# Low-rank products, the first router and the scan matrix in another order at a kernel's start

## The chip, the cores and the metric

The kernel runs on one core of a Trainium2 chip. The metric is the device time of one execution in microseconds; the median of three runs before is 432.93 us (432.88 to 433.32). One further execution was taken with the profiler; all rows below are of it. Engines are called TensorE (PE, and PEld for its weight loads), VectorE (DVE), ScalarE (ACT), GpSimd (POOL) and SyncE (SP).

## The reference, cut to what matters

```python
xn = layernorm(x)                                    # x: 8 x 256 x 256, float32
x = x + attn0(xn) + ffn0(xn)
xn = layernorm(x)
x = x + attn1(xn) + ffn1(xn)

# ffn0: 8 experts, every one on every token; experts 0 and 1 have a low-rank part
gate = einsum('btd,edf->ebtf', xn, Wg);  up = einsum('btd,edf->ebtf', xn, Wu)
gate[:2] += einsum('btd,edr,erf->ebtf', xn, Ga, Gb)  # the same for up with Ua, Ub; r = 64
mid = silu(gate) * up
out = einsum('ebtf,efd->ebtd', mid, Wd)              # down, with Da, Db for experts 0 and 1
ffn0 = einsum('bte,ebtd->btd', router_weights(xn), out)

# attn0: z = xn @ W.T ; h = z + sum_k eta_k * scan(lam_k, z) ; layernorm(h) * gamma + beta
# router_weights: distance of a sigmoid from 1/e, exponentials, a fallback to the best two
```
attn1 is a gated linear attention with a group norm, ffn1 picks two of 8 experts by token.

## The kernel before

2048 tokens are worked in four groups of 512. All 37 matrices of 256x256 stay in SBUF. For float32 accuracy each is split in two parts: ScalarE copies `w_raw` into the high part `w_hi` (`high`, line 1081), and GpSimd subtracts it to get the low part `w_lo` (`split_low`, line 541, one instruction of 512 columns for each matrix; VectorE does it for the first two, `vector_low`). `w_lo` lies in the place of `w_raw`. Each product is then three matmuls for each piece of the contraction (`passes`, L698). Activations are split likewise: `x_high`/`x_low`, `mid_high`/`mid_low`.

Within a group TensorE runs over e = 0 to 7 (experts in the order 2, 3, 4, 5, 6, 7, 0, 1). `gate_up(g, e, [c])` makes half c of gate and up, 12 matmuls of 512 columns, in PSUM banks G0, U0 or G1, U1. ScalarE applies silu (`silu`), VectorE multiplies by up (`mid_mul`), ScalarE and VectorE split the result (`mid_high`, `mid_low`), and `down(g, e - 1)` runs after `gate_up(g, e)`, 24 matmuls of 256 columns in D0, D1. VectorE adds it, weighted by the router's weight, to `rows` (`down_add`).

Low-rank parts are added to the weights: `lora(i)` (L707) multiplies the two factors into a PSUM bank, VectorE adds that to `w_raw` (`add_lora`, L1750), and only then ScalarE makes the high part. i = 0, 1 (gate0, up0) stand after gate and up of e = 2 in TensorE's stream, i = 2, 3 (gate1, up1) after e = 3, i = 4, 5 (down0, down1) after e = 4; all in M0, M1.

The attention scan of the first layer is a product with a 256-column matrix that VectorE builds at the start of the kernel in four steps (`make_scan_matrix`, each a scan L1714 and a multiply-add L1716, and at the end a cast and a low part): steps 0, 1 ahead of the first `mid_mul`, steps 2, 3 at e = 3. `scan_input` (after `down(0, 4)`) waits for all `lora_added`, `scan` follows at e = 6. `toep_made` marks the matrix done; SyncE's queue waits for it and then loads gamma and clears `sorted_rows` in nine transfers (L454, L459).

At the start TensorE runs 20 warm-up matmuls (L939), transposes x (L719), makes gate and up of the first half in one go (`first_gate_up`, L765 to L771), then the second half, then the router's product (`router_start`, L727), whose transposes (`router_end`, L734) stand in e = 1. VectorE's routing chain (`route_start`, `route_middle`, `route_best`, `route_end`) stands behind `mid_low(0, 0)`. GpSimd's splits are paced by marks: two after x is normed, three after the first part of the scan matrix (`powers_made`), one after `mid_mul` of e = 1, six after `routed`, then beta is added to rows (L560), which waits for `down_add` of e = 2, then six splits, then eight after the next group's x is normed (`x_norm(1)`, at e = 4 on VectorE).

Every engine works its instructions in the order written; the order is by hand, with a semaphore for each step. SyncE's queue issues the transfers of `CHUNKS` in order.

## Time and profile before

| | us |
|---|---|
| median of 3 runs | 432.93 |
| lowest, highest | 432.88, 433.32 |
| the profiled execution's own time | 432.74 |
| its span, first to last instruction | 431.0 |
| TensorE busy | 424.1 |
| VectorE busy | 347.4 |
| ScalarE busy | 177.9 |
| GpSimd busy | 166.2 |

Busy times are sums over the whole span and hide where an engine is the limit. TensorE's are modelled at their ends, so a short stall between two matmuls can't be seen in them; the starts of its weight loads show it.

### The profile page before, as it was taken

The page shows a single profiled execution, that of the slowest core. Times are in us where ns is not written, and L with a number is a line of the kernel's source. Part 1 is how long each engine was busy: PE and PEld are TensorE (multiplying, and loading weights), DVE is VectorE, ACT ScalarE, POOL GpSimd, SP SyncE. Part 2 cuts the span into 40 slices and gives each one's busy share as a digit, 9 for nine tenths or more (in the row PEclk, how much of TensorE's full clock was granted, in tenths as well). Part 3 has the DMA queues.
Part 4 walks back from the last instruction along what each step waited for, and adds up shares of the span by engine and source line. Part 5 has one row for each costly group of instructions (what it writes and reads, how often), then busy time and mean ns, then how long its engine had stood idle before and what let it go on. Part 6 is the DMA issues. An engine that isn't in the chain of part 4 may idle for free.

```text
span 431.0 us, 7493 instructions
## 1 busy us (share of the span) xinstructions
PE 424.1 (98%) x2520; PEld 369.8 (86%) x2520; DVE 347.4 (81%) x1090; ACT 177.9 (41%) x333; POOL 166.2 (39%) x198
## 2 busy tenths in 40 slices
PE   7999999999999999999999999999999999999997
PEld 5788889887888898978988989788999889999886
DVE  6787899998899669889996687989979465856785
ACT  5445445424253725441356234322733333525130
POOL 2417379351017200701072905210441054654656
PEclk9999999999999999999999999999999999999999
DMA  8992499970002130000020310000110844521398
GB/s 286 292 420 92 133 295 285 298 192 0 2 10 89 27 121 1 2 2 1 2 79 19 100 50 0 2 1 2 49 51 24 236 156 122 159 102 50 111 229 261
DMA packets 30166, 46.89 MB, mean 109 GB/s; under 512 B 2680, under 2 KB 24464, under 8 KB 29488
## 3 DMA queue, kind: packets, MB, share of 16 engines
q1 hardware_dynamic: 26064, 36.80, 28.3%
q0 software_dynamic: 3072, 8.80, 6.6%
q10 hardware_dynamic: 992, 0.81, 0.6%
q8 instruction: 21, 0.34, 0.3%
q14 instruction: 17, 0.14, 0.1%
HBM read 22.74 MB, written 23.65 MB: 108 GB/s over the span
## 4 chain that ended last, share of the span: by engine, by line
PE 96%; DVE 2%; DMA 1%; ACT 0%; issue 0%; DVEq 0%
PE D L698 28%; PE G L698 25%; PE U L698 25%; PE M L698 10%; PE M L707 1%; PE D L727 1%; PE M L849 1%; PE M L824 1%; DMA rows<-x 1%; PE M L719 1%; PE D L734 0%; PE M L932 0%; DVE w_lo L1355 0%; DVE stats L1365 0%; PE M L918 0%
## 5 line engine op out<-in xcount | busy, mean ns | idle before, releaser
L698 PE MATMUL D<-w_hi,mid_hi 128*128 128x256 f32 x260 | 74.3, 286 | 0.0
L698 PE MATMUL D<-w_hi,mid_lo 128*128 128x256 f32 x260 | 73.6, 283 | 0.0
L698 PE MATMUL D<-w_lo,mid_hi 128*128 128x256 f32 x260 | 73.5, 283 | 0.0
L1103 ACT ACTIVATE mid<-G 128x512 f32<-128x512 f32 x64 | 37.9, 595 | 76.4 <-PE G L698 66.1
L1476 DVE TENSOR_TENSOR mid<-mid,U 128x512 f32<-128x512 f32 x64 | 43.3, 684 | 25.9 <-PE U L698 14.6
L1490 DVE SCALAR_TENSOR_TENSOR rows<-D,weight,rows 128x256 f32<-128x256 f32 x128 | 54.0, 476 | 4.4 <-PE D L698 4.1
L545 POOL TENSOR_TENSOR w_lo<-w_raw,w_hi 128x512 fp32r<-128x512 f32 x35 | 46.9, 1370 | 27.0 <-ACT w_hi L1076 18.6
L1076 ACT ACTIVATE mid_hi<-mid 128x512 fp32r<-128x512 f32 x64 | 39.9, 630 | 37.5 <-DVE mid L1476 37.2
L1355 DVE TENSOR_TENSOR mid_lo<-mid,mid_hi 128x512 fp32r<-128x512 f32 x64 | 48.3, 774 | 6.1 <-ACT mid_hi L1076 4.6
L698 PEld LDWEIGHTS D<-w_hi,mid_hi 128*128 128x128 f32 x260 | 49.8, 191 | 1.7 <-issue 1.0
L698 PEld LDWEIGHTS D<-w_lo,mid_hi 128*128 128x128 f32 x260 | 49.8, 192 | 0.7
L698 PE MATMUL G<-xT_hi,w_hi 128*128 128x512 f32 x126 | 50.4, 400 | 0.0
L698 PEld LDWEIGHTS D<-w_hi,mid_lo 128*128 128x128 f32 x260 | 49.8, 192 | 0.0
L698 PE MATMUL U<-xT_hi,w_hi 128*128 128x512 f32 x126 | 49.4, 392 | 0.0
L698 PE MATMUL G<-xT_lo,w_hi 128*128 128x512 f32 x126 | 49.3, 392 | 0.0
L698 PE MATMUL G<-xT_hi,w_lo 128*128 128x512 f32 x126 | 49.1, 390 | 0.0
L698 PE MATMUL U<-xT_hi,w_lo 128*128 128x512 f32 x126 | 49.1, 389 | 0.0
L698 PE MATMUL U<-xT_lo,w_hi 128*128 128x512 f32 x126 | 49.0, 389 | 0.0
L625 POOL DMA_INDIRECT sorted_rows<-weighted,slots x24 | 25.2, 1051 | 54.3 <-ACT weighted L1181 48.8
L582 POOL TENSOR_TENSOR scan_part<-scan_part,gamma 128x256 f32<-128x256 f32 x16 | 11.7, 765 | 64.6 <-ACT scan_part L1129 64.6
L698 PEld LDWEIGHTS G<-xT_hi,w_lo 128*128 128x128 f32 x126 | 23.7, 188 | 5.2
L698 PEld LDWEIGHTS U<-xT_hi,w_hi 128*128 128x128 f32 x126 | 23.6, 188 | 5.0
(360 smaller groups left out, 956.4 us busy)
## 6 DMA issues: line engine op xcount, KB each, us to landing
sorted_rows<-weighted SPq DMA_DIRECT2D x8, 1542.0 KB, 18.8
w_raw<-weights SPq DMA_DIRECT2D x5, 1024.0 KB, 18.1
stage<-sorted_rows SPq DMA_DIRECT2D x31, 128.5 KB, 2.3
w_raw<-weights SPq DMA_DIRECT2D x3, 768.0 KB, 11.8
rows<-x SPq DMA_DIRECT2D x7, 256.0 KB, 3.1
part<-rows SPq DMA_DIRECT2D x12, 128.0 KB, 2.0
sums_gate<-part SPq DMA_DIRECT2D x3, 512.0 KB, 6.0
fetched<-returned SPq DMA_DIRECT2D x3, 512.0 KB, 4.8
```

The source lines that it names most:

```text
L545: nc.gpsimd.tensor_tensor(flat, w_raw[:, n, :], w_hi[:, n, :, :].rearrange("p k d -> p (k d)").bitcast(F32), ALU.subtract).then_inc(pool_l ...
L582: nc.gpsimd.tensor_tensor(scan_part[:, t, :], scan_part[:, t, :], gamma[:, :], ALU.mult)\
L625: nc.gpsimd.indirect_dma_start(sorted_rows[:, :], bass.IndirectOffsetOnAxis(slots[:, q, j:j + 1], 0), weighted[j][:, t, :], None).then_inc ...
L698: ins = nc.tensor.matmul(out_ap, a, b, start=(first and n == 0), stop=(last and n == 3 * len(pairs) - 1))
L707: ins = nc.tensor.matmul(LORA_PS[i][:, k * D:(k + 1) * D], a[:, k * P:(k + 1) * P], b, start=True, stop=True)
L719: ins = nc.tensor.transpose(MT[k][:, t * P:(t + 1) * P], ln[:, t, k * P:(k + 1) * P], ident[:, :])
L727: ins = nc.tensor.matmul(bank[0:2 * E, :], routers[:, layer, k, :, :].rearrange("p a e -> p (a e)"), part[:, k, :], start=n == 0, stop=n = ...
L1076: return nc.scalar.activation(o, i, ACT.Copy)
L1103: nc.scalar.activation(mid[:, c, :], GU[2 * c][:, :], ACT.Silu).then_inc(silu_ready, 1)
L1355: return v.tensor_tensor(o, i, hi.bitcast(F32), ALU.subtract)
L1476: v.tensor_tensor(mid[:, c, :], mid[:, c, :], GU[2 * c + 1][:, :], ALU.mult)\
L1490: ins = v.scalar_tensor_tensor(rows[g % 2][:, t, :], DN[t // 2][:, (t % 2) * D:(t % 2 + 1) * D], weight0[:, t, ORDER[e]:ORDER[e] + 1], row ...
```

## The change

TensorE runs 12 warm-ups, then the low-rank products i = 0 to 3 into G1, U1, D0, D1. ScalarE copies them from there into `w_raw` (`hold_lora`), and GpSimd's queue adds the weights onto them by two accumulating transfers. VectorE's adds remain for i = 4, 5, now both at e = 5 as before; the products of down stay after e = 4 on TensorE. The factors of gate and up are loaded ahead of the weights. The first router's product stands between first gate and first up product, its transposes behind the up product. VectorE's routing chain up to `route_best` stands ahead of `mid_low(0, 0)`; the scan matrix is made at e = 3 (steps 0, 1) and e = 4 (steps 2, 3). GpSimd's splits: 2, 3, 4; the two transfers; 5, 6 after `route_best` (`picks_made`); 7 to 13 after `routed`; beta; 14 to 17; 18 on after x of the next group is normed.

```diff
-CHUNKS = ((0, 1), (1, 2), (2, 4), (4, 5), (5, 8), (8, 10), (10, 13), (13, 17), (17, 21), (21, 25), (25, 28),
-          (28, 32), (32, 36), (36, 37))
+LORA_HELD = 4
+JOINED = tuple((WHERE[f"gate{_e}"], WHERE[f"gate{_e}"] + 2) for _e in range(2))
+CHUNKS = ((0, 1), (1, 2), (2, 4), (4, 5), (5, 8), (8, 10), (10, 13), (13, JOINED[0][0]), JOINED[0],
+          (JOINED[0][1], JOINED[1][0]), JOINED[1], (JOINED[1][1], 28), (28, 32), (32, 36), (36, 37))
-WARMUPS = 20
+WARMUPS = 12
-        LORA_PS = [M0, M1, M0, M1, M0, M1]
+        LORA_PS = [G1, U1, D0, D1, M0, M1]
@@ SyncE
             load_x(sp, 0, 0)
+            load_gu(0)
+            load_gu(1)
             for c in range(6):
                 load_chunk(c)
...
             for c in range(7, len(CHUNKS)):
-                load_chunk(c)
+                if CHUNKS[c] not in JOINED:
+                    load_chunk(c)
@@ GpSimd
             pool.wait_ge(xn_act_ready, 2)
             split_low(2, 4)
-            pool.wait_ge(powers_made, 1)
-            split_low(4, 7)
-            pool.wait_ge(mid_ready, at(0, 2 * E, 2 * 1 + 2))
-            split_low(7, 8)
+            split_low(4, 5)
+            for e in range(2):
+                first, end = JOINED[e]
+                pool.wait_ge(lora_held, 2 * (e + 1))
+                nc.gpsimd.dma_start(w_raw[:, first:end, :], weights[:, first:end, :], accum_op=ALU.add)\
+                    .then_inc(chunk_loaded[CHUNK_OF[first]], 16)
+            pool.wait_ge(picks_made, 1)
+            split_low(5, 7)
             pool.wait_ge(routed, 1)
-            split_low(8, 14)
+            split_low(7, 14)
...
-            split_low(14, 20)
+            split_low(14, 18)
             pool.wait_ge(xn_ready, at(1, 2, 2))
-            split_low(20, WHERE["o"])
+            split_low(18, WHERE["o"])
@@ TensorE
+            for i in range(LORA_HELD):
+                if i % 2 == 0:
+                    pe.wait_ge(lora_gu_loaded[i // 2], 16)
+                lora(i)
             pe.wait_ge(const_made, 5)
             transpose_x(0)
-            first_gate_up()
-            gate_up(0, 0, [1])
+            first_product(0)
             pe.wait_ge(routers_ready, 1)
             router_start(M0, 0, xT_hi, xT_lo, (logitT_ps[0], 1))
+            first_product(1)
+            router_end(M0, 0, 0)
+            pe.wait_ge(lora_held, 2)
+            gate_up(0, 0, [1])
...
-                    if g == 0 and e == 1:
-                        router_end(M0, 0, 0)
...
-                    if g == 0 and e == 2:
-                        pe.wait_ge(logit0_ready, 1)
-                        pe.wait_ge(lora_gu_loaded[0], 16)
-                        for i in (0, 1):
-                            lora(i)
-                    if g == 0 and e == 3:
...
+                    if g == 0 and e == 1:
+                        pe.wait_ge(lora_held, LORA_HELD)
...
                     if e == SCAN_AT[g]:
-                        pe.wait_ge(lora_added, LORA)
+                        pe.wait_ge(lora_added, LORA - LORA_HELD)
@@ ScalarE
+            def hold_lora(i):
+                act.wait_ge(lora_ps, i + 1)
+                copy(w_raw[:, WHERE[LORA_NAMES[i]], :], LORA_PS[i][:, :]).then_inc(lora_held, 1)
...
             high(0)
+            x_norm(0)
             high(1)
-            x_norm(0)
+            x_high(0)
             high(2)
-            x_high(0)
             high(3)
+            hold_lora(0)
             silu(0, 0, 0, mid_used=False)
+            hold_lora(1)
+            logits_out(0, 0)
             high(4)
+            hold_lora(2)
+            hold_lora(3)
+            route_start(0)
+            silu(0, 0, 1, mid_used=False)
+            route_exp(0)
             high(5)
-            silu(0, 0, 1, mid_used=False)
             high(6)
-            logits_out(0, 0)
             for c in range(KC):
                 mid_high(0, 0, c)
-            route_start(0)
             silu(0, 1, 0)
-            route_exp(0)
@@ VectorE
             vector_low(1)
-            make_scan_matrix((0, 1))
             mid_mul(0, 0, [0])
+            route_start(0, M0)
+            route_middle(0)
             mid_mul(0, 0, [1])
+            route_best(0)
+            v.memset(carrier[:, :], 0.0).then_inc(picks_made, 1)
             mid_low(0, 0)
-            route_start(0, M0)
             mid_mul(0, 1, [0])
-            route_middle(0)
-            route_best(0)
             mid_mul(0, 1, [1])
...
-                        if first and e in (3, 4, 5):
-                            add_lora(2 * e - 6)
-                            add_lora(2 * e - 5)
+                        if first and e == 5:
+                            for i in range(LORA_HELD, LORA):
+                                add_lora(i)
...
-                    if g and e == 1:
+                    if e == 1:
                         route_end(g)
...
-                    if first and e == 1:
-                        route_end(g)
...
-                    if first and e == 3:
-                        make_scan_matrix((2, 3))
+                    if first and e in (3, 4):
+                        make_scan_matrix((2 * e - 6, 2 * e - 5))
```

## Rows read from the trace of the kernel before

**Rows 1.** The page, its part 1: busy time, share of the span, instructions.
```profile
PE 424.1 (98%) x2520; PEld 369.8 (86%) x2520; DVE 347.4 (81%) x1090; ACT 177.9 (41%) x333; POOL 166.2 (39%) x198
```

**Rows 2.** Waits of TensorE, 0 to 110 us: total us, times, longest.
```profile
PE U L768 <- DVE w_lo L1355: 0.5, 1, 0.5
```

**Rows 3.** Timeline of weight loads: start us, us, instruction, idle before.
```profile
31.40 0.19 PEld L698 LDWEIGHTS U<-xT_lo,w_hi 128*128 128x128 f32 x1
31.63 0.19 PEld L698 LDWEIGHTS U<-xT_hi,w_lo 128*128 128x128 f32 x1
32.17 1.59 PEld L707 LDWEIGHTS M<-gu_factors 64*128 64x128 f32 x8 [0.35 <-issue]
34.09 0.19 PEld L698 LDWEIGHTS D<-w_hi,mid_hi 128*128 128x128 f32 x1 [0.33 <-issue]
...
42.63 1.59 PEld L707 LDWEIGHTS M<-gu_factors 64*128 64x128 f32 x8 [0.35 <-issue]
```

**Rows 4.** Timeline of all engines, 0 to 14 us.
```profile
1.53 6.46 PE L939 MATMUL D<-xT_lo 128*128 128x512 f32 x20 [1.53 <-DVE xT_lo L1757]
...
7.24 0.63 ACT L1076 ACTIVATE w_hi<-w_raw 128x512 fp32r<-128x512 f32 x1 [0.73 <-DMA w_raw<-weights]
...
7.94 1.09 ACT L1136 ACTIVATE ln<-rows,shift,rstd 128x256 f32<-128x256 f32 x2
...
10.19 0.96 PE L765 MATMUL G<-xT_hi,w_hi 128*128 128x512 f32 x2 [0.34 <-ACT xT_hi L1076]
...
11.28 1.69 DVE L1355 TENSOR_TENSOR w_lo<-w_raw,w_hi 128x512 fp32r<-128x512 f32 x1
```

**Rows 5.** DMA issues: KB each, us to landing; first one issued at 1.34.
```profile
w_raw<-weights SPq DMA_DIRECT2D x1, 256.0 KB, 4.0
...
sums_gate<-returned POOLq DMA_DIRECT2D x3, 512.0 KB, 10.7
```

**Rows 6.** Timeline of VectorE, first and last instruction of the choosing part.
```profile
23.76 0.20 DVE L1438 TENSOR_SCALAR den_e<-th_e 128x64 f32<-128x64 f32 x1 [0.41 <-ACT th_e L1123]
...
26.80 0.23 DVE L1407 TENSOR_TENSOR picked<-expert_id,top_f 128x64 f32<-128x64 f32 x1
```

**Rows 7.** Timeline of VectorE, 42 to 89 us.
```profile
42.81 0.69 DVE L1476 TENSOR_TENSOR mid<-mid,U 128x512 f32<-128x512 f32 x1 [0.71 <-PE U L698]
...
44.80 0.69 DVE L1714 TENSOR_TENSOR_SCAN carry_gain<-small_in,carry_gain 128x256 f32<-128x256 f32 x1
...
47.62 0.42 DVE L1355 TENSOR_TENSOR toep_lo<-gamma,toep_hi 128x256 fp32r<-128x256 f32 x1
...
50.55 0.69 DVE L1476 TENSOR_TENSOR mid<-mid,U 128x512 f32<-128x512 f32 x1 [0.93 <-PE U L698]
51.15 1.28 DVE L1750 TENSOR_TENSOR w_raw<-w_raw,M 128x512 f32<-128x512 f32 x2
...
54.25 3.07 DVE L1355 TENSOR_TENSOR mid_lo<-mid,mid_hi 128x512 fp32r<-128x512 f32 x2
...
59.79 1.21 DVE L1330 TENSOR_SCALAR rstd<-newton 128x4 int32<-128x4 int32 x1
...
73.22 1.61 DVE L1735 TENSOR_TENSOR_SCAN carry_gain<-small_in 128x255 f32<-128x255 f32 x1
...
87.84 0.68 DVE L1355 TENSOR_TENSOR mid_lo<-mid,mid_hi 128x512 fp32r<-128x512 f32 x1
```

**Rows 8.** Timeline of weight loads: the first of the last down product.
```profile
88.70 0.19 PEld L698 LDWEIGHTS D<-w_hi,mid_hi 128*128 128x128 f32 x1
```

**Rows 9.** Timeline of GpSimd, 50 to 75 us: the two batches of splits.
```profile
52.54 8.44 POOL L545 TENSOR_TENSOR w_lo<-w_raw,w_hi 128x512 fp32r<-128x512 f32 x6
63.31 10.97 POOL L545 TENSOR_TENSOR w_lo<-w_raw,w_hi 128x512 fp32r<-128x512 f32 x8 [2.34 <-DVE ln L1375]
```

**Rows 10.** Timeline of SyncE's queue and of ScalarE: clearing transfers, first use.
```profile
48.46 40.19 SPq L459 DMA_DIRECT2D sorted_rows<-weighted  x9
...
125.69 2.07 ACT L1181 ACTIVATE weighted<-rows,row_shift,row_gain 128x256 f32<-128x256 f32 x4
```

More of the change, by code:

```diff
@@ L755, in scan, with first_product @@
                                   (*now, yT_hi[:, 1, :], yT_lo[:, 1, :])]).then_inc(h_ps, 1)
-            def first_gate_up():
-                for up in range(2):
-                    n = WHERE[NAMES[up]]
-                    cols = slice(0, P)
-                    for k in range(KC):
-                        pe.wait_ge(high_ready, n + 1)
-                        pe.wait_ge(xT_hi_ready, k + 1)
-                        nc.tensor.matmul(GU[up][:, :], w_hi[:, n, k, cols], xT_hi[:, k, :], start=k == 0, stop=False)
-                    for k in range(KC):
-                        pe.wait_ge(vector_low_ready, n + 1)
-                        nc.tensor.matmul(GU[up][:, :], w_lo[:, n, k, cols], xT_hi[:, k, :], start=False, stop=False)
-                    for k in range(KC):
-                        pe.wait_ge(xT_lo_ready, k + 1)
-                        ins = nc.tensor.matmul(GU[up][:, :], w_hi[:, n, k, cols], xT_lo[:, k, :], start=False,
-                                               stop=k == KC - 1)
-                    ins.then_inc(gu_ps, 1)
+            def first_product(up):
+                n = WHERE[NAMES[up]]
+                cols = slice(0, P)
+                for k in range(KC):
+                    pe.wait_ge(high_ready, n + 1)
+                    pe.wait_ge(xT_hi_ready, k + 1)
+                    nc.tensor.matmul(GU[up][:, :], w_hi[:, n, k, cols], xT_hi[:, k, :], start=k == 0, stop=False)
+                for k in range(KC):
+                    pe.wait_ge(vector_low_ready, n + 1)
+                    nc.tensor.matmul(GU[up][:, :], w_lo[:, n, k, cols], xT_hi[:, k, :], start=False, stop=False)
+                for k in range(KC):
+                    pe.wait_ge(xT_lo_ready, k + 1)
+                    ins = nc.tensor.matmul(GU[up][:, :], w_hi[:, n, k, cols], xT_lo[:, k, :], start=False,
+                                           stop=k == KC - 1)
+                ins.then_inc(gu_ps, 1)
             def gate_up(g, e, chunks=range(KC), between=None):
@@ L938, in _ @@
             for _ in range(WARMUPS):
-                nc.tensor.matmul(D1[:, :], xT_lo[:, 0, 0:P], xT_lo[:, 0, :], start=True, stop=True)
+                nc.tensor.matmul(M0[:, :], xT_lo[:, 0, 0:P], xT_lo[:, 0, :], start=True, stop=True)
+            for i in range(LORA_HELD):
+                if i % 2 == 0:
+                    pe.wait_ge(lora_gu_loaded[i // 2], 16)
+                lora(i)
             pe.wait_ge(const_made, 5)
             transpose_x(0)
-            first_gate_up()
-            gate_up(0, 0, [1])
+            first_product(0)
             pe.wait_ge(routers_ready, 1)
             router_start(M0, 0, xT_hi, xT_lo, (logitT_ps[0], 1))
+            first_product(1)
+            router_end(M0, 0, 0)
+            pe.wait_ge(lora_held, 2)
+            gate_up(0, 0, [1])
             def unit(u, owners):
@@ L976, in group @@
                         scan(g)
-                    if g == 0 and e == 2:
-                        pe.wait_ge(logit0_ready, 1)
-                        pe.wait_ge(lora_gu_loaded[0], 16)
-                        for i in (0, 1):
-                            lora(i)
-                    if g == 0 and e == 3:
-                        pe.wait_ge(lora_added, 2)
-                        pe.wait_ge(lora_gu_loaded[1], 16)
-                        for i in (2, 3):
-                            lora(i)
-                    if g == 0 and e == 4:
-                        pe.wait_ge(lora_added, 4)
-                        pe.wait_ge(lora_down_loaded, 16)
-                        for i in (4, 5):
-                            lora(i)
+                    if g == 0 and e == 1:
+                        pe.wait_ge(lora_held, LORA_HELD)
                     if e == 1:
                         pe.wait_ge(logit0_ready, at(g, 1, 1))
+                    if g == 0 and e == 4:
+                        pe.wait_ge(lora_down_loaded, 16)
+                        for i in range(LORA_HELD, LORA):
+                            lora(i)
                     if g and e == 3:
@@ L1717, in make_scan_matrix @@
                                                  gamma[:, :] if k else unit, ALU.mult, ALU.add))
-                if SCANS - 1 not in scans:
-                    v.memset(carrier[:, :], 0.0).then_inc(powers_made, 1)
-                else:
+                if SCANS - 1 in scans:
                     setup(v.tensor_copy(toep_hi[:, :], gamma[:, :]))
@@ L1782, in group @@
                             unit_low(0)
-                        if first and e in (3, 4, 5):
-                            add_lora(2 * e - 6)
-                            add_lora(2 * e - 5)
+                        if first and e == 5:
+                            for i in range(LORA_HELD, LORA):
+                                add_lora(i)
                         if first and e == NORM_AT[g]:
```

9 lines of the change are left out of this document (4 added, 5 removed).

## The prediction

> **What bounds the kernel now.** I read the page first: TensorE is busy for 424.1 of 431.0 us, 98%, the others for 81% and less [rows 1]. So an edit gains only by what it takes out of TensorE's own stream, or out of a wait of TensorE. The list of waits of TensorE over the first 110 us, read next, holds four entries, all before 14 us; the one the change aims at is the wait of the first up product for its low part [rows 2]. Then the weight loads in order of time: in dense stretches they follow at 0.23 us for 512 columns with no hole (31.40, 31.63) [rows 3], and this is how a stall is seen, since a matmul's modelled end hides it. Last, VectorE beside GpSimd from 42 to 89 us. There VectorE is idle only once, for 0.93 us, and its last low part of the last expert ends at 88.52, 0.18 us ahead of the down product that needs it at 88.70 [rows 7, 8]. VectorE is thus a second bound, just hidden, in the very stretch from which the change takes TensorE work.
>
> **Low-rank products of gate and up put first.** They stand in the dense stream now: a last product load at 31.63, the eight passes from 32.17, the next down product at 34.09. That is 2.46 us where 0.23 would do, so 2.23 us a time; the second time has the same shape, 1.59 us of loads after a 0.35 us hole [rows 3]. Both go: **-4.46 us** of TensorE. The third pair (down) stays.
>
> **The head.** Warm-ups fall from 20 (1.53 to 7.99) to 12, so they end near 7.99 - 8 x 0.227 = 6.2 [rows 4]. The factors are now loaded ahead of the first two weight chunks and should land where these did, 1.34 + 4.0 = 5.3 and 7.24 [rows 4, 5]; the four products, 16 passes of 0.2 to 0.23, run from about 6.4 to 9.8. The first chunk, two places later in the queue, lands near 7.9, so ScalarE's norm ends at 9.55 instead of 9.03, and then the eight transposes wait for TensorE itself: the first matmul moves from 10.19 to 11.2 (between 10.6 and 11.6). On the other side the wait in the up product goes: its low part came at 12.97, late because VectorE needed 1.69 us for an instruction that takes 0.68 elsewhere [rows 2, 4, 7], a hole of 0.8 us together with its refill. The router's four matmuls now fill it. Head: +1.0 - 0.8 = **+0.2** (-0.4 to +0.7). If the products were free and nothing else moved, the sum would be -4.26. The copies that hold the products (four of 0.6 on ScalarE, as its copy at 7.24 in [rows 4]) fit between its other work: the logits copy ends at 14.8, the router's transposes come at 15.2.
>
> **Weights added by DMA.** The two transfers of 512 KB from GpSimd's queue are like the three late ones, which landed in 10.7 us [rows 5]; issued near 17 they may take twice that under the weight loads and are wanted by ScalarE near 45. Nothing, and 1 to 1.5 us of GpSimd while it would wait anyway. They spare VectorE four adds of 0.64.
>
> **Routing chain ahead.** Let T be the start of the first expert's second half on TensorE. Its 12 matmuls take 2.7, VectorE starts 0.5 after the last (42.81 against a stream that ended 0.31 ahead of 42.63, by the hole in [rows 3]), multiplies 0.6, and runs the choosing part, now in front of the low parts: 23.76 to 27.03, 3.3 us [rows 6]. Then two low parts of 0.65: T+8.4. TensorE wants them after 36 matmuls, T+8.2. So 0.3 us are lost even undisturbed. But the mark that lets GpSimd go on is set right before them, and GpSimd's next split takes its turn between the two: +1.03, the time VectorE stood still behind one split at 59.79 (1.21 for an instruction of 0.17) [rows 7]. **+1.35** (0 to 2.4: with the first also blocked). In the kernel before this chain stood behind the low parts.
>
> **The scan matrix moved.** This is the term that decides. Start the clock when the fourth expert's up product is through: VectorE starts at 42.81, TensorE needs the last low part at 88.70. TensorE's distance, 45.89, becomes 45.89 - 2.23 = **43.66**, since the second pair of products stood right behind that point. VectorE's way, 42.81 to 88.52, is 45.71. Out of it come the 0.93 of idle time and one pair of adds, 1.28 (the pair before lies ahead of 42.81) [rows 7]. The second half of the scan matrix, 44.80 to 47.96 or 3.16, moves one expert later; the first half takes its place and came from the head: 3.16 less the casts plus one small step, 2.68. Undisturbed VectorE needs 45.71 - 0.93 - 1.28 + 2.68 = 46.2 and meets TensorE's 43.7: 2.5 us late, with 0.1 of slack in between.
>
> **Turns with GpSimd.** From [rows 7] I take a rule of this trace: while GpSimd runs its splits back to back, a VectorE instruction on two SBUF operands waits for the split in progress, then GpSimd waits its turn. Two low parts took 3.07 for 1.28, a small step 1.21, a scan over 255 columns 1.61 for 0.69. Products read from PSUM did not wait (the adds of products, 1.28 for two, beside GpSimd's beta sum). Before, the batch of six splits [rows 9] cost VectorE 1.8 in the low parts and 1.2 in the norm. Now it is four splits, and they meet the low parts and the moved half of the scan matrix, eight such instructions in a row: 0.25 + 4 x 1.03 = 4.4, against 3.0: +1.4. The second batch grows from eight [rows 9] to ten, and reaches into the carry gain's last step and the next low parts: +1.3. Together +2.7; the bounds are -1.7 (the moved scans don't wait, four of the waits gone, the second batch as before) and +4. So VectorE arrives 2.5 + 2.7 = **5.2 us** late (0.8 to 6.5). TensorE would pay it mostly in front of the scan's input product, which waits until VectorE has added the two down products, and the rest at the last down product.
> The rows show turns. The Trainium skill ("SBUF — State Buffer", SBUF: two separate sides) states it as an exclusive lock on a pair of ports, held for a whole instruction, against VectorE work with two SBUF inputs or in a two-port mode; it speaks against moving scans beside the splits. By that rule the sum stands as above; were it not so, the term would be 2.5 or less.
>
> **Behind the scan matrix on SyncE's queue**: its mark comes near 60 instead of 48, and the clearing transfers wait for it. They are issued from 48.46 for 40.19 us and end near 102; now near 114. ScalarE first needs them at 125.69 [rows 10]. Nothing; if the margin of 11 us were gone, as much as it is overrun.
>
> **Sum**: -4.46 + 0.2 + 1.35 + 5.2 = +2.3. The profiled execution took 432.74 (431.0 of span and 1.7 around it), the median of the runs is 432.93, so it is a usual one: 432.74 + 2.3 = **435.0**.
>
> **Rivals.**
> First, that is the case above: VectorE and its turns set group 0's end. For it: one idle time in 46 us; the 0.18 us at 88.52. Chance 0.48, 433.8 to 437.
> Second, **the turns don't grow**, the change is faster. Place: the low parts and the moved scans, 50 to 58 us. Price: with the contention of before less the norm's 1.2, VectorE is 1.3 late, the first low parts cost 0.3: -4.46 + 0.2 + 0.3 + 1.3 = -2.7, 430.1; with contention simply unchanged 2.5 and -1.5, 431.3. It decides once VectorE's extra waiting stays under 0.9 us in all. For it: the splits are held back until the norm is done. Against: scans waited at 73.22. Chance 0.27.
> Third, between them: half of the added waiting, the low parts as costed: -4.46 + 0.2 + 1.35 + 3.5 = +0.6, 433.3. Chance 0.16.
> Fourth, **no stall at all**, VectorE had hidden slack: -4.26, 428.5. Against it the idle time of 0.93. Chance 0.04.
> Fifth, the head goes wrong: the factors land late, TensorE stands between the shorter warm-ups and the products, and runs the first products at 1.2 instead of 2.4 GHz. The warm-ups stood 0.32 apart on average where dense matmuls of their size stand 0.227 apart [rows 3, 4]; some 12 matmuls at half the pace cost 12 x 0.227 = 2.7 more, 437.7. Chance 0.05.
>
> **How the numbers follow.** 0.2% of the time, 0.87 us, is about what a measurement can tell from no change: faster is below 432.1, slower above 433.8. Faster takes the second and fourth and a little of the third, 0.32; same 0.18; slower 0.50, the first and fifth less a margin. For 8 in 10 the range leaves out the fourth and the far end of the fifth: 430.2 to 437.0. The likeliest case alone is 433.8 to 437.0.
>
> **What would show each step.** The passes of the low-rank products before 10 us, none at 32 and 42. The first product's start near 11.2 and no hole in the up product. A hole of about 1.3 us in front of the first down product (near 24) and a wait of it for VectorE's low parts. Scan instructions of 1.3 to 1.7 us instead of 0.7 between 50 and 60; a wait of the scan's input product of 2 to 3 us for VectorE's adds; later a second one at the last down product. VectorE without idle time from there to 90. I am wrong if TensorE's stream has no holes after 15 us, or if VectorE's scans keep 0.69.

## The result, and the profile after

| | before | after |
|---|---|---|
| median of the runs, us | 433.02 (432.85 to 433.45, 8 runs) | 435.42 (434.75 to 436.93, 8 runs) |
| ratio to before | | 1.0061 (95%: 1.0044 to 1.0077) |
| the profiled execution, its span | 432.74, 431.0 | 436.93, 435.1 |

The change makes the kernel slower by 0.6%. The forecast was 435.0. The profiled execution of the changed kernel is the slowest of its runs. Five of its runs lie at 434.75 to 435.54 and three at 436.43 to 436.93; the difference has a place in the trace, shown at the end of this section.

The page, part 1 (busy time, share of the span, instructions): TensorE is busy 1.0 us less than in [rows 1], in a span 4.1 us longer.

```profile
PE 423.1 (97%) x2512; PEld 369.7 (85%) x2512; DVE 348.8 (80%) x1086; ACT 179.8 (41%) x337; POOL 172.1 (40%) x200
```

Waits of TensorE, 0 to 110 us (total us, times, longest), against [rows 2]. The wait of the up product for its low part is gone. Waits for VectorE's low parts and for its added weights, 5.5 us together, stand in its place.

```profile
PE D L706 <- DVE mid_lo L1365: 3.2, 2, 2.1
PE M L706 <- DVE w_raw L1758: 2.3, 1, 2.3
```

Timeline of weight loads (start us, us, instruction, idle before), against [rows 3] and [rows 8]:

```profile
6.75 0.73 PEld L715 LDWEIGHTS G<-gu_factors 64*128 64x128 f32 x4 [0.45 <-issue]
...
8.26 1.05 PEld L715 LDWEIGHTS D<-gu_factors 64*128 64x128 f32 x5
9.64 0.85 PEld L727 LDWEIGHTS M<-ident,ln 128*128 128x128 f32 x8 [0.33 <-issue]
11.04 0.19 PEld L771 LDWEIGHTS G<-xT_hi,w_hi 128*128 128x128 f32 x1 [0.55 <-issue]
...
23.37 0.19 PEld L706 LDWEIGHTS U<-xT_hi,w_lo 128*128 128x128 f32 x1
25.04 0.19 PEld L706 LDWEIGHTS D<-w_hi,mid_hi 128*128 128x128 f32 x1 [1.48 <-issue]
...
63.34 0.19 PEld L706 LDWEIGHTS D<-w_hi,mid_lo 128*128 128x128 f32 x1
66.05 0.19 PEld L706 LDWEIGHTS M<-w_hi,xT_hi 128*128 128x128 f32 x1 [2.52 <-DVE w_raw L1758]
...
87.75 0.90 PEld L727 LDWEIGHTS M<-ident,ln 128*128 128x128 f32 x8
90.96 0.19 PEld L706 LDWEIGHTS D<-w_hi,mid_hi 128*128 128x128 f32 x1 [2.32 <-issue]
```

The four low-rank products of gate and up stand in front of the transposes now, and none of them is in the dense stream. Three long holes are new. Read from the load before to the load behind, less one spacing (0.23 for 512 columns, 0.12 in a down product, 0.87 for the eight transposes, which is the distance when nothing waits), they are 25.04 - 23.37 - 0.23 = 1.44 at the first down product, 66.05 - 63.34 - 0.12 = 2.59 at the scan's input product, and 90.96 - 87.75 - 0.87 = 2.34 at the last down product. Two small ones of 0.21 and 0.22 stand at 60.61 and 84.88.

Timeline of VectorE, against [rows 7], and below it the splits of GpSimd, against [rows 9]:

```profile
22.54 0.69 DVE L1365 TENSOR_TENSOR mid_lo<-mid,mid_hi 128x512 fp32r<-128x512 f32 x1
23.15 1.77 DVE L1365 TENSOR_TENSOR mid_lo<-mid,mid_hi 128x512 fp32r<-128x512 f32 x1
...
42.09 0.69 DVE L1486 TENSOR_TENSOR mid<-mid,U 128x512 f32<-128x512 f32 x1 [2.03 <-PE U L706]
...
51.03 2.60 DVE L1365 TENSOR_TENSOR mid_lo<-mid,mid_hi 128x512 fp32r<-128x512 f32 x2
53.55 1.78 DVE L1724 TENSOR_TENSOR_SCAN carry_gain<-small_in,carry_gain 128x256 f32<-128x256 f32 x1
55.37 1.33 DVE L1726 SCALAR_TENSOR_TENSOR gamma<-carry_gain,small_in,gamma 128x256 f32<-128x256 f32 x1
56.73 1.66 DVE L1724 TENSOR_TENSOR_SCAN carry_gain<-small_in,carry_gain 128x256 f32<-128x256 f32 x1
58.43 0.48 DVE L1726 SCALAR_TENSOR_TENSOR gamma<-carry_gain,small_in,gamma 128x256 f32<-128x256 f32 x1
...
64.72 1.28 DVE L1758 TENSOR_TENSOR w_raw<-w_raw,M 128x512 f32<-128x512 f32 x2
...
78.41 1.83 DVE L1365 TENSOR_TENSOR mid_lo<-mid,mid_hi 128x512 fp32r<-128x512 f32 x2
...
90.21 0.68 DVE L1365 TENSOR_TENSOR mid_lo<-mid,mid_hi 128x512 fp32r<-128x512 f32 x1
```

```profile
22.70 3.37 POOL L549 TENSOR_TENSOR w_lo<-w_raw,w_hi 128x512 fp32r<-128x512 f32 x2 [4.43 <-DVE carrier L1779]
...
51.34 6.51 POOL L549 TENSOR_TENSOR w_lo<-w_raw,w_hi 128x512 fp32r<-128x512 f32 x4
64.29 13.85 POOL L549 TENSOR_TENSOR w_lo<-w_raw,w_hi 128x512 fp32r<-128x512 f32 x10 [6.45 <-DVE ln L1385]
```

A low part of 0.69 takes 1.77 while GpSimd's first split runs (22.70), scans of 0.69 take 1.78 and 1.66, a multiply-add of 0.48 takes 1.33. The multiply-add at 58.43, just behind the batch of four (51.34 + 6.51 = 57.85), takes its bare 0.48.

Last, the granted clock, by stretches (length, then busy time of TensorE, its loads, VectorE, ScalarE and GpSimd, then the clock as a share of 2.4 GHz, DMA share, GB/s). First the profiled execution above, then another one of the same kernel, which took 434.67 us (it is the first run of the next section).

```profile
85.00:90.00 5.00, 3.88 (x33) 3.64 (x32) 4.78 (x10) 3.78 (x9) 2.99 (x4) 1.00 1.10 264
90.00:95.00 5.00, 4.01 (x22) 4.04 (x23) 4.47 (x10) 0.35 (x1) 4.56 (x7) 0.68 1.10 273
```

```profile
65.00:70.00 5.00, 4.55 (x25) 4.56 (x26) 5.00 (x9) 2.21 (x4) 5.00 (x4) 0.66 1.13 259
...
90.00:95.00 5.00, 4.60 (x32) 4.34 (x33) 4.93 (x12) 0.43 (x2) 5.00 (x7) 1.00 1.13 259
```

In both, a piece of a 5 us stretch runs at 1.2 instead of 2.4 GHz, right behind a hole. In the first execution it lies behind the last hole: the last down product runs from 90.96 to 95.31, 4.35 us, where the other execution needs 2.86 (90.37 to 93.23). In the second it lies behind the hole of the scan's input product, where VectorE is the bound: TensorE only arrives later at the last hole, which shrinks from 2.34 to 0.96. The mean granted clock over a whole run is on record for every run: 0.995 or 0.996 in all twelve of the changed kernel. So the clock falls in each of them, and what sets the two groups apart is, as it seems, where it falls; the place is traced in these two only.

### The profile page after: what moved, and what is told of

Same layout as the page of the kernel before. It is cut to its first block, busy times and chain, and to the rows that moved or that the text cites. A ratio compares the mean times of both kernels' runs of the same rounds, so it can differ in the third digit from the quotient of the medians.

```text
span 435.1 us, 7473 instructions
## 1 busy us (share of the span) xinstructions
PE 423.1 (97%) x2512; PEld 369.7 (85%) x2512; DVE 348.8 (80%) x1086; ACT 179.8 (41%) x337; POOL 172.1 (40%) x200
## 4 chain that ended last, share of the span: by engine, by line
PE 86%; DVE 12%; issue 1%; ACT 1%; DVEq 0%
PE D L706 25%; PE G L706 21%; PE U L706 21%; PE M L706 8%; DVE mid_lo L1365 2%; DVE rows L1500 2%; PE D L735 1%; PE M L945 1%; DVE mid L1486 1%; PE M L855 1%; DVE carry_gain L1724 1%; PE M L830 1%; DVE gamma L1726 1%; DVE carry_gain L1743 1%; PE M L727 1%
## 5 line engine op out<-in xcount | busy, mean ns | idle before, releaser
L549 POOL TENSOR_TENSOR w_lo<-w_raw,w_hi 128x512 fp32r<-128x512 f32 x35 | 50.1, 1464 | 25.6 <-ACT w_hi L1078 11.4
L1365 DVE TENSOR_TENSOR mid_lo<-mid,mid_hi 128x512 fp32r<-128x512 f32 x64 | 50.4, 808 | 4.7 <-ACT mid_hi L1078 3.3
```

Source lines behind the costliest of these rows:

```text
L549: nc.gpsimd.tensor_tensor(flat, w_raw[:, n, :], w_hi[:, n, :, :].rearrange("p k d -> p (k d)").bitcast(F32), ALU.subtract).then_inc(pool_l ...
L1365: return v.tensor_tensor(o, i, hi.bitcast(F32), ALU.subtract)
```

## The experiments

Every median below stands beside runs of the kernel before on the same chip; these lay between 433.07 and 433.12, except for the last kernel. Each ratio is to them, with its 95% interval in brackets. Where an expectation gives the last hole as 1.6 to 1.8, that was counted with too wide a spacing for the transposes; by the spacing of 0.87 used above it is 2.34.

**The changed kernel once more.** No edit.

> The changed kernel once more, nothing edited. Theory A (VectorE sets the end of group 0, through its own work and its turns with GpSimd): holes of 1.4 us before the first down product, 2.6 before the scan's input product and 1.8 before the last down product, in this trace too, within 0.1 each. Theory B, about the spread of the runs (434.75 to 436.93): the granted clock fell behind the last hole in the profiled run (0.68 over 90 to 95 us, where the last down product took 4.3 us instead of 2.9), a dip of some executions only. Then a run near 435 shows the same holes without that dip, and one near 436.8 shows it; the two kinds lie about 1.5 us apart.

435.59 us (434.65 to 436.61), 1.0064 [1.0041, 1.0088]. The holes are those above: 1.44, 2.59, and at the end

```profile
88.54 0.90 PEld L727 LDWEIGHTS M<-ident,ln 128*128 128x128 f32 x8
...
90.37 0.19 PEld L706 LDWEIGHTS D<-w_hi,mid_hi 128*128 128x128 f32 x1 [0.93 <-issue]
```

The result repeats, with two runs at 434.7 and two at 436.5. I had expected a run near 435 to have no fall of the clock and the same last hole. It has the fall, behind the scan's input product, and a smaller last hole (0.96).

**The scan matrix away from GpSimd's splits.** All four steps in the fourth expert, the first two ahead of its low parts.

```
+                        if first and e == 3:
+                            make_scan_matrix((0, 1))
...
-                    if first and e in (3, 4):
-                        make_scan_matrix((2 * e - 6, 2 * e - 5))
+                    if first and e == 3:
+                        make_scan_matrix((2, 3))
```

> The changed kernel with the scan matrix one place earlier: steps 0 and 1 between the two halves of the fourth expert (e = 3), where VectorE stood idle for 2.0 us, steps 2 and 3 behind that expert's low parts, as in the kernel before. Theory A: VectorE gets back 3.2 us at e = 4 and three waits for splits of about 1 us each, and is late by some 0.6 us at the start; the holes before the scan's input and the last down product shrink from 4.6 together to 0.5 or less, and the time falls by 4 to 5.5 us to 430 to 431.4. Rival C (the holes come from the added products' wait or the second batch of splits, whichever place the matrix has): the first of them may go, the one before the last down product stays near 1.8, and the time stays above 433.

432.82 us (432.1 to 433.3), 0.9992 [0.9982, 1.0001]. That is 2.8 less than the changed kernel, from the order of the same instructions alone. Timeline of VectorE, and the loads at the last down product:

```profile
45.30 0.68 DVE L1724 TENSOR_TENSOR_SCAN carry_gain<-small_in,carry_gain 128x256 f32<-128x256 f32 x1
46.02 0.48 DVE L1726 SCALAR_TENSOR_TENSOR gamma<-carry_gain,small_in,gamma 128x256 f32<-128x256 f32 x1
```

```profile
85.18 0.90 PEld L727 LDWEIGHTS M<-ident,ln 128*128 128x128 f32 x8
88.03 0.19 PEld L706 LDWEIGHTS D<-w_hi,mid_hi 128*128 128x128 f32 x1 [1.95 <-issue]
```

The steps have their bare times and the hole of 2.59 is gone. But the last hole still stands at 1.98: TensorE arrives there 2.6 us sooner (transposes at 85.18, in the changed kernel at 87.75), and VectorE 2.9 (the load at 88.03, there at 90.96). From the weights it adds at the scan's input to its last low part VectorE needs 25.0 us here (63.00 to 87.96), 24.9 in the changed kernel (66.00 to 90.89) and 23.5 in the kernel before (65.02 to 88.52). That stretch is the one beside the second batch of splits, ten where [rows 9] has eight, and this run leaves it alone. So the gain at the scan's input is carried to the end of the group whole, and what was lost behind it stays lost; I had expected 1.4 to 2.8 us more. In all ten runs the mean clock is 0.999 or 1.0: the fall is absent.

**The low parts ahead of the choosing part.** The first low parts in front of the routing chain.

```
             mid_mul(0, 0, [1])
+            mid_low(0, 0)
             route_best(0)
             v.memset(carrier[:, :], 0.0).then_inc(picks_made, 1)
-            mid_low(0, 0)
```

> The changed kernel with the low parts of the first expert ahead of the choosing part of the routing chain, as in the kernel before; all else as changed. Theory A: the hole of 1.4 us before the first down product goes, the rest keeps its size, since VectorE has 4 us of idle time at e = 3 to start the scan stretch afresh: -1.4, near 434.0. Rival C (the time that this hole cost is made up by later holes, for VectorE is the bound from the start on): the later holes grow by as much and the time stays at 435.4.

435.62 us (434.18 to 436.37), 1.005 [1.0032, 1.0068], where 434.0 was expected. The 1.44 went, and a hole of 0.87 came one product later:

```profile
32.48 0.19 PEld L706 LDWEIGHTS D<-w_hi,mid_hi 128*128 128x128 f32 x1 [0.92 <-issue]
```

Here half of the idle time is a wait for the adds of the first down product (0.5), which need the routing weights. The chain is wanted as early as the low parts are, and neither order serves both. The scan hole (idle 2.52) and the last (2.31) stayed. The 0.6 us less of holes can't be seen in the median of five runs that spread over 2.2.

**Splits 5 and 6 held until the first low parts are through.**

```
             pool.wait_ge(picks_made, 1)
+            pool.wait_ge(mid_lo_ready, 2)
             split_low(5, 7)
```

> The changed kernel with GpSimd's splits 5 and 6 held until VectorE's low parts of the first expert are done; VectorE's and TensorE's order untouched. It prices the turn in the first hole. Theory A: the second low part, 1.77 us in the changed kernel, takes 0.69 again and the hole before the first down product falls from 1.4 to 0.3 to 0.4. The time falls by up to 1.1, less what the later splits cost in route_end (a wait of about 1 us as in the kernel before, covered by VectorE's idle time at e = 3). 434.3 to 435. Rival D (low parts are slow for another cause): 1.77 stays.

434.70 us (434.21 to 435.7), 1.0036 [1.0023, 1.0048]. The first hole falls from 1.44 to 0.34, with one of 0.31 at the next down product: both low parts take 0.69. So 1.1 of the 1.44 was the one turn of GpSimd, as the prediction split it (1.03 and 0.3).

**Two of the four splits held until the scan matrix is done.**

```
-            split_low(14, 18)
+            split_low(14, 16)
+            pool.wait_ge(toep_made, 1)
+            split_low(16, 18)
```

> The changed kernel with GpSimd's last two splits before the norm (14 to 17 in one batch now) held until the scan matrix is done; VectorE's order is untouched. It prices the turns alone. Theory A: two of the three waits of 0.9 to 1.1 us in the moved scan steps go, VectorE's scan ends about 2 us earlier and the hole before the scan's input product falls from 2.6 to 0.6 to 1.0; -2 us, 433.3 to 433.7. Rival D (the long scan instructions have another cause, memory traffic of the weight loads say, or the splits only move into the norm and cost as much there): scans stay at 1.3 to 1.8 us or the norm's small steps lengthen, and the time stays within 0.5 of 435.4.

434.71 us (434.41 to 435.42), 1.0036 [1.0023, 1.0048]. Timeline of VectorE:

```profile
53.49 1.78 DVE L1726 TENSOR_TENSOR_SCAN carry_gain<-small_in,carry_gain 128x256 f32<-128x256 f32 x1
...
55.83 0.69 DVE L1726 TENSOR_TENSOR_SCAN carry_gain<-small_in,carry_gain 128x256 f32<-128x256 f32 x1
...
59.73 0.75 DVE L1341 TENSOR_SCALAR newton<-mv 128x4 f32<-128x4 f32 x1
```

Two waits are gone (0.85 and 0.97), one of 0.58 comes back in the norm. The hole at the scan's input product falls from 2.59 to 1.43, where 0.6 to 1.0 was expected; the last one does not move (idle 2.31). The time falls by 0.9, not by 2.

**The scan matrix alone moved**, in the kernel before, low-rank products where they were.

```
-            make_scan_matrix((0, 1))
+            v.memset(carrier[:, :], 0.0).then_inc(powers_made, 1)
...
-                    if first and e == 3:
-                        make_scan_matrix((2, 3))
+                    if first and e in (3, 4):
+                        make_scan_matrix((2 * e - 6, 2 * e - 5))
```

> The other part alone: the kernel before with only the scan matrix moved, steps 0 and 1 to e = 3 and 2 and 3 to e = 4, the low-rank products left where they were. Theory A: VectorE has 2.7 us more before 88.5 and 1.0 us of idle time and slack to put it in, and three to four waits of about 1 us more for splits in the moved scans; the last down product waits 3 to 5 us. The head may give back up to 0.3. 435.5 to 437.5. Rival C (scans are absorbed, the bound lies elsewhere): within 0.5 of the kernel before.

437.55 us (437.42 to 437.9), 1.0103 [1.0086, 1.012]. One load of its trace:

```profile
69.42 0.19 PEld L698 LDWEIGHTS M<-w_hi,xT_hi 128*128 128x128 f32 x1 [2.52 <-DVE w_raw L1748]
```

With nothing taken out of TensorE's stream it is 4.5 us slower, just above the 435.5 to 437.5 that were expected. There are holes of 0.6 and 2.60, and behind the second the clock falls (0.66 of full over 70 to 75 us). The last down product's transposes start at 92.54 and it has no hole of its own; it is 4.7 later than before (93.41 against 88.70 in [rows 8]). The fall as such is not the cause: the one run of the four with a mean clock of 1.0 took 437.42, the others 437.52 to 437.9. VectorE is the bound there, so a TensorE that runs on at full clock would, as it seems, only have waited at the end.

**The low-rank products alone**, with the router's product, the routing chain, the scan matrix and the pacing of GpSimd's splits in the order of before. The lines below are TensorE's and VectorE's.

```
             first_product(0)
+            first_product(1)
+            pe.wait_ge(lora_held, 2)
+            gate_up(0, 0, [1])
             pe.wait_ge(routers_ready, 1)
             router_start(M0, 0, xT_hi, xT_lo, (logitT_ps[0], 1))
...
+            make_scan_matrix((0, 1))
             mid_mul(0, 0, [0])
             mid_mul(0, 0, [1])
             mid_low(0, 0)
             route_start(0, M0)
```

> One part alone: the low-rank products first, held and joined by DMA, with the factors loaded first and 12 warm-ups as in the changed kernel; the router, its chain, the scan matrix and GpSimd's pacing stand as in the kernel before. Theory A (the products' 4.46 us are a real gain, eaten by VectorE's new place for the scan matrix and the routing chain): VectorE's way from the fourth expert on is 45.7 - 0.9 - 1.3 = 43.5, TensorE's 43.7, so no later hole over 0.3 us; the head costs 0.9 to 1.3 with the up product's wait still there. -3.2 to -3.6 against the kernel before: 429.5 to 430. Rival C (VectorE is the bound whatever stands in the head, so a TensorE gain comes back as a hole): a hole of over 1.5 us before the last down product and 431.5 or more.

435.37 us (434.82 to 435.78), 1.0057 [1.004, 1.0074]: slower than before by 2.3, where I had expected it 3.2 to 3.6 faster. It is my largest miss in these runs. TensorE's longest wait, and the rows around it:

```profile
PE D L707 <- DVE rows L1502: 2.4, 1, 2.4
```

```profile
36.05 0.19 PEld L707 LDWEIGHTS D<-w_hi,mid_hi 128*128 128x128 f32 x1 [2.80 <-issue]
```

```profile
25.76 0.20 DVE L1450 TENSOR_SCALAR den_e<-th_e 128x64 f32<-128x64 f32 x1 [0.42 <-ACT th_e L1131]
...
34.83 0.19 DVE L1476 TENSOR_TENSOR weight<-th_e,sums 128x32 f32<-128x32 f32 x1
35.05 1.27 DVE L1502 SCALAR_TENSOR_TENSOR rows<-D,weight,rows 128x256 f32<-128x256 f32 x3
```

The routing chain runs on VectorE from 25.76 to 35.0. Only then can the first down product be added, and only then is its PSUM tile free for the second. The 2.23 us of products that stood ahead of the second down product [rows 3] had covered that chain: in the kernel before VectorE starts the adds at 33.06 and TensorE loads at 34.09, one us behind them as here. Without the products and with a chain ended at the same time, TensorE would have waited from 31.86, 2.2 us. Here the chain ends 2.0 later and TensorE arrives only 1.4 later, which makes it 2.76. The 1.4 is the head with the products in front and the up product's wait (0.97) still there: the second half of e = 1 starts at 22.32, before at 20.89. Further holes are 0.76 at the scan's input and 1.04 at the last down product. Together -4.46 + 1.43 + 4.56 = +1.5, and the last down product starts 1.62 later than before (90.32); the rest of the 2.3 was not followed. So this part has no value without the routing chain brought forward. That the forward chain has its place only if the scan matrix leaves the head is argued; no run has the one without the other. Alone the parts cost 2.3 and 4.5 us, together 2.4.

**Spread.** One step of the scan matrix at the end of the third expert, two between the halves of the fourth, one behind its low parts; splits 14 and 15 made with 7 to 13, in GpSimd's idle time; splits 5 and 6 held.

```
-            split_low(7, 14)
+            split_low(7, 16)
...
-            split_low(14, 18)
+            split_low(16, 18)
```

> The changed kernel with the work laid into VectorE's and GpSimd's idle time: scan step 0 at the end of e = 2, steps 1 and 2 between the halves of e = 3, step 3 and the casts behind the low parts of e = 3; splits 14 and 15 right behind 13 instead of behind beta; splits 5 and 6 behind the first low parts. Theory A: the first hole is 0.4, the scan's input product waits for nothing, the last down product 0.5 or less (the second batch of splits still costs 1.3 more than before): 430 to 431. Rival C: the last hole stays over 1 us, as in the run with the matrix one place earlier (1.7): 431.5 to 432.5.

433.41 us (431.9 to 434.11), 1.0004 [0.9991, 1.0017], where 430 to 431 was expected. In its profiled execution of 432.19 only small holes (0.24 to 0.36) stand ahead of the last down product, and that one still has 2.34. The ten runs fall into two groups, and the mean granted clock tells them apart: four at 431.9 to 432.58 with 1.0, six at 433.34 to 434.11 with 0.996. Their medians, 432.35 and 433.82, put the price of the fall at 1.5 us here.

**GpSimd's later splits taken out of the changed kernel.** A fill with zeros, which reads nothing, stands for each split from 14 on, so the output lacks these low parts.

```
+                nc.gpsimd.memset(w_lo[:, n, :, :].rearrange("p k d -> p (k d)").bitcast(F32), 0.0).then_inc(pool_low_ready, 1)
...
-            split_low(14, 18)
+            for n in range(14, 18):
+                mark_low(n)
```

> The changed kernel; GpSimd's splits from number 14 on are not computed, a fill with zeros of the same tile, without a source, stands in their place (the output lacks these low parts, TensorE's work keeps its shape). It measures the turns by themselves. Theory of the prediction (VectorE's own work makes it about 2.5 us late, the turns 2.7 more): scans of 0.69, low parts of 0.69 each, the hole at the scan's input product falls from 2.59 to 0.3 or less and the one at the last down product goes: 430.5 to 431.4. Rival (VectorE's own added work is what stalls TensorE, turns are incidental): holes stay over 2 us in all, 433.5 to 435. If a fill also bars VectorE, scans stay above 0.69 and the run tells nothing.

430.2 us (429.63 to 430.23), 0.9934 [0.9919, 0.9949]. Timeline of VectorE, then the loads at the last down product:

```profile
51.87 0.68 DVE L1730 TENSOR_TENSOR_SCAN carry_gain<-small_in,carry_gain 128x256 f32<-128x256 f32 x1
...
53.11 0.69 DVE L1730 TENSOR_TENSOR_SCAN carry_gain<-small_in,carry_gain 128x256 f32<-128x256 f32 x1
...
71.52 0.69 DVE L1492 TENSOR_TENSOR mid<-mid,U 128x512 f32<-128x512 f32 x1 [1.04 <-PE U L712]
```

```profile
84.40 0.90 PEld L733 LDWEIGHTS M<-ident,ln 128*128 128x128 f32 x8
85.27 0.19 PEld L712 LDWEIGHTS D<-w_hi,mid_hi 128*128 128x128 f32 x1
```

The scans stand where the change put them and keep 0.68 and 0.69. All holes behind 30 us are gone; the only one left is the first, 1.43, whose splits were kept. VectorE waits for TensorE again (71.52). This settles that the later holes need the turns with GpSimd: the moved work by itself makes none. It does not show that the moved work is free. The run takes out all turns of these batches, also those that the kernel before had, and with those and without the moved work the kernel before had no hole either. Holes come of both together.

**The carry gain late**, on the spread order: its first piece to the end of the seventh expert, the second behind the group.

```
-                    if first and e in (5, 6):
-                        make_carry_gain(e - 5)
+                    if first and e == 6:
+                        make_carry_gain(0)
...
                     gates_start(g)
+                    if first:
+                        make_carry_gain(1)
```

> On top of the spread scan matrix and the held splits: the carry gain, two pieces of VectorE work that stood at the ends of the sixth and seventh experts of group 0 (5.3 us with its waits, and 1.9 us), is moved: the first piece to the end of the seventh, the second behind the group, ahead of the attention step. Theory (VectorE is continuously busy, so each microsecond taken out ahead of the last down product shortens that product's wait of 1.61): some 4 to 5 us of VectorE leave, the last hole goes whole, the earlier holes stay (0.34, 0.31, 0.36, 0.24): 431.0 to 431.8, and no clock dip behind 88, since no long hole is left to stand ahead of it. Rival (the low parts there are late for another reason, or the late piece delays the routing or attention step of the next group): 433.4, or a new hole near 100.

431.75 us (431.02 to 431.86), 0.9966 [0.9954, 0.9978]: 1.3 us faster than the kernel before, which the changed one trails by 2.4. The last hole is 1.98 (86.83, idle 1.96), only 0.36 less, yet the clock's fall is absent: the mean clock is 0.999 or 1.0 in all six runs. Of the 1.7 us that it gained over the median of the spread order, 0.6 is left against the four runs of that order without the fall.

**The early scan matrix with the same two edits** (splits 5 and 6 held, carry gain late).

> The scan matrix early (two steps between the halves of the fourth expert, two behind its low parts), splits 5 and 6 held until the first low parts, carry gain late as in the kernel above. Theory: of the 432.8 that the early scan matrix alone took, 0.8 goes at the first down product (1.43 becomes 0.34 and 0.31) and 1.7 at the last: 430.4 to 431.2, faster than both kernels. Rival (each hole comes back elsewhere, or the clock dip follows the next longest hole): 432.3 to 433.

431.87 us (431.06 to 432.01), 0.9965 [0.9951, 0.9979]. As good, not better: the last hole is 1.51, and small ones of 0.3 to 0.5 stand at four places. Expected was 430.4 to 431.2.

**Both pieces of the carry gain behind the group**, on the spread order.

> As the kernel with the carry gain late, but both pieces of it stand behind group 0, ahead of the attention step. In the run before, the first piece took 3.0 us (80.31 to 83.3) ahead of the last low parts, and the last down product still had a hole of 1.25. Theory (VectorE's continuous work is all that makes that hole): it goes, 431.75 less 1.25 is 430.5, 430.2 to 430.9, with the small holes left as they are. Rival (VectorE behind the group has no room for 2.2 us more; the carry gain delays the attention step and the routing of the next group): the hole goes and one of about its size comes in group 1, 431.3 to 432.

442.52 us (439.85 to 442.98) beside 443.72 (441.83 to 444.79) of the kernel before: 0.9975 [0.9956, 0.9993]. It ran on another chip, on which this kernel and the kernel before take some 10 us more than their like elsewhere. In the trace nearly all of that lies behind 350 us, so only the ratio and the first part are used. There the last down product's loads follow the transposes by 0.87, without a hole. In group 1 a new wait stands ahead of its moments:

```profile
130.37 0.38 PE L917 MATMUL M<-mv_g,bias_raw 128*128 128x2 f32 x2 [1.21 <-DVE mv_g L1671]
```

Both theories had a part: 1.98 gone, 1.21 given back. Whether it beats the two kernels above stays open, as they were not run on the same chip.

## Why the prediction was right, point by point

**Low-rank products out of the stream, -4.46.** Right. The loads at 32 and 42 us are gone and no hole took their place there. That this holds only with the routing chain forward, the products alone show (+2.3); the prediction did not see it and costed this part as if it stood by itself.

**Head, +0.2.** The shape was right: products from 6.75 (expected 6.4), first matmul's load at 11.04 (expected 11.2), no hole in the up product. The products were cheaper than costed (6.75 to 9.31, not 6.4 to 9.8). The transposes follow them by the 0.33 that stands behind such products in [rows 3] too, so they waited for TensorE, as forecast. The second half of expert 1 starts at 20.87, where before had 20.89: 0.0 in this execution, 0.6 less in the other one.

**First down product, +1.35.** Measured 1.44, from the cause given: one turn of GpSimd between the two low parts (0.69 and 1.77), 1.1 of it by the held splits, which left 0.34. The forecast's own ends, T+8.4 and T+8.2, give 0.2 for that rest, not the 0.3 it names.

**Scan matrix and turns, +5.2 (0.8 to 6.5).** Measured 0.21 + 2.59 + 0.22 + 2.34 = 5.36. The places are those forecast, most at the scan's input product and the rest at the last down product, though the shares are nearly equal. The waits inside the first batch are 1.3 in the low parts, 1.09, 0.85 and 0.97 in the scan steps, 4.2 together against 4.4 forecast. VectorE has no idle time from 51 until 93.37. One word was wrong: the 46.2 us that the forecast calls undisturbed hold the waits that [rows 7] already had. With no turns at all VectorE is not late anywhere (no hole behind 30 us). So 2.5 is what the moved work adds on top of the old waits, and 2.7 what the new order adds to the waits, and read like this both fit. The forecast's way of VectorE, 42.81 to 88.52 or 45.71 us, is 42.09 to 90.89 or 48.80 us in the changed kernel. That is 3.09 more, and 0.93 of idle time went, so 4.02 more of work and waits. Own work is 2.68 - 1.28 = 1.40 of it by the forecast's terms, and 2.62 is left for added waits, against 2.7. The end of the adds divides it (66.00 above; in the kernel before 65.02, by the line below): 1.23 ahead of it, forecast 1.4, and 1.39 behind, beside the ten splits, forecast 1.3.

```profile
63.74 1.28 DVE L1750 TENSOR_TENSOR w_raw<-w_raw,M 128x512 f32<-128x512 f32 x2
```

The Trainium skill ("SBUF — State Buffer", SBUF: two separate sides) has the rule that decided the sign: one pair of ports, held by one engine for a whole instruction. The runs agree, with up to 1.1 us more for an instruction beside splits of 1.4 to 1.6, and none beside a fill, which by the same section does not lock out VectorE's work on two inputs, since it reads no SBUF.

**SyncE's queue.** Right: the clearing transfers follow the late mark, from 60.12, and nothing waits for them.

**The sum.** -4.46 + 0.0 + 1.44 + 5.36 = +2.34, where +2.3 was forecast. The profiled execution is 4.19 slower than that of before. 1.5 is the clock behind the last hole (4.35 less 2.86), and 0.6 lies behind 409 us and was not followed: the first matmul of the last group's moments starts at 405.91 before and at 409.50 after, 3.59 later. The chain 2.34 + 1.5 = 3.8 meets that within 0.3. The median, 435.42, belongs to the lower group of runs. If the fall lies in all of that group where it lies in the traced execution of 434.67, behind the scan's hole, it costs them next to nothing, since TensorE waits at the last hole anyway, and the head (0.0 and 0.6 less in the two traces) makes the rest of their spread; this is argued from one trace. **So the median lies near the forecast for the right reason, with a small share of luck**: no term stands for a fall of the clock at the holes, and had it come behind the last hole in most runs, the median would be near 436.8. I had such a fall as a rival, but in the head, where the granted clock stayed at full.

**The rivals.** The turns did grow, by 2.6, against the second and the third (half of the waiting). The third's own sum was off: 2.5 and half of 2.7 are 3.85, not 3.5, so its price is 433.7. The fourth falls with the holes.

## What to carry to other kernels

Where two engines share a port and take turns, count for each step that is moved how many of its instructions fall beside the other engine's batch. Three instructions of the scan steps, bare elsewhere, cost 0.9 to 1.1 us more each here, and making the four steps 3.5 to 8.3 us earlier gave 2.8 us back without a change in work. An operation that looks like waste on the bounding engine can be the cover of another engine's chain, so ask of every removed step which chain it was waiting alongside. And where the second bound, VectorE here, has no idle time between two holes, each hole stands for its own stretch: closing the first carries its gain to the end but does not shrink the last one.

## What the runs showed of the hardware that was not expected

A hole of 2.3 to 2.6 us in TensorE's stream can be followed, within a microsecond of its end, by a stretch at 1.2 GHz that costs 1.2 to 1.5 us of a down product (4.06 to 4.36 us in four profiled executions, where 2.86 is bare). It does not come each time: the same hole of 2.34 was followed by it at 90.96 in the changed kernel and not at 87.43 in the spread one, and it took the scan's hole (granted clock 0.66 over 65 to 70) in place of the last one in another execution of the changed kernel. The mean clock of the runs, those on the last chip left out, gives the counts: 0.995 or 0.996, so a fall somewhere, in 36 of 47 runs of kernels whose longest traced hole is 2.3 to 2.8, and 0.999 or 1.0 in all 25 runs of the four kernels whose longest is 1.43 to 1.98. Two of the 42 runs of the kernel before that stand beside them, a kernel without such a hole, show a lower clock too (0.995 and 0.998, at 433.98 and 434.02). What decides was not tried. So a hole's price in a median is its length and a share of that stretch, and the stretch costs only where TensorE is the bound behind it.

A wait behind GpSimd's split also strikes small instructions (0.75 for a step of 0.17 in the norm) and scans of which one operand is a column repeated (1.78 and 1.66). It did not strike the adds of products, which read PSUM (64.72: 1.28 for two, beside the batch that starts at 64.29).
